# Cross-attention latent queries: from float32 matmuls to three float32r matmuls on split operands, with a new order in the loop

## The reference

```python
def _L1_xattn_ref(hidden_q, kv_c, Wq, w_kc_q, w_kc_kv, W_qr, W_kr, Wo):
    B, S, L = (2, 128, 128)
    DIM_Q, H, K, D_C, D_CQ, R = (256, 16, 128, 64, 192, 64)
    ...
    q_hk = (hidden_q @ Wq.T).reshape(Bv, Sv, H, K)
    q_big = jnp.einsum('bshk,hkq->bshq', q_hk, w_kc_q)
    ...
    q_big = _apply_rope(q_big, sin_q[None, :, None, :], cos_q[None, :, None, :])
    ...
    kv_r = _apply_rope(kv_c, sin_k[None], cos_k[None])
    q_r = jnp.einsum('bshq,hqr->bhsr', q_big, W_qr)
    k_r = jnp.einsum('bld,hdr->bhlr', kv_r, W_kr)
    scores = jnp.einsum('bhsr,bhlr->bhsl', q_r, k_r)
    attn = jax.nn.softmax(scores, axis=-1)
    ctx_c = jnp.einsum('bhsl,bld->bhsd', attn, kv_r)
    ctx_lat = jnp.einsum('bhsd,hkd->bhsk', ctx_c, w_kc_kv)
    ctx = ctx_lat.transpose(0, 2, 1, 3).reshape(Bv, Sv, H * K)
    return ctx @ Wo.T
```

## Time and profile before

| | |
|---|---|
| median of 3 runs | 1042.09 us (1037.66 to 1042.62) |
| profiled execution | 1034.71 us, its span 1032.9 us |
| PE busy in the span | 947.3 us (92%) |
| DVE, ACT, POOL busy | 633.0 us (61%), 437.7 us (42%), 113.8 us (11%) |
| mean granted clock of TensorE | 0.967 |
| latent-query matmuls | 384 records, 92.4 us |
| cross-attention set-up and loop | about 518 to 806 us of the span |

### The profile page before, as it was taken

One profiled execution on the slowest core, in us unless ns is written; L12 is line 12 of the kernel. 1 busy time (PEld: TensorE's weight loads), 2 busy tenths in 40 slices (PEclk: granted clock), 3 DMA queues, 4 the chain that ended last, 5 costly groups with the idle time before them and its releaser, 6 DMA issues.

```text
span 1032.9 us, 14127 instructions
## 1 busy us (share of the span) xinstructions
PE 947.3 (92%) x5344; PEld 735.2 (71%) x5344; DVE 633.0 (61%) x1222; ACT 437.7 (42%) x1036; POOL 113.8 (11%) x126
## 2 busy tenths in 40 slices
PE   5999779999999988888788999999998799999998
PEld 4666457888888777656476777777775578888886
DVE  4357655666566553455566867868776456666664
ACT  4722443433334313666534444434444533334432
POOL 1300000000000046000031322222221000000000
PEclk9989869999999989988999999999999899999999
DMA  5000031111110040000060000000000312111101
GB/s 215 1 2 1 1 109 46 46 51 56 46 30 1 0 163 1 2 1 2 1 275 1 2 1 1 2 1 1 2 1 1 122 33 62 47 46 46 30 1 41
DMA packets 12089, 38.37 MB, mean 37 GB/s; under 512 B 1888, under 2 KB 3968, under 8 KB 11136
## 3 DMA queue, kind: packets, MB, share of 16 engines
q1 hardware_dynamic: 12000, 37.60, 10.7%
q0 software_dynamic: 32, 0.01, 0.0%
HBM read 36.55 MB, written 1.05 MB: 36 GB/s over the span
## 4 chain that ended last, share of the span: by engine, by line
PE 73%; ACT 8%; DVE 5%; issue 1%; POOL 0%; DVEq 0%
PE ps L1005 68%; ACT Q L840 3%; PE ps L1455 2%; PE ps L1110 1%; DVE nm L482 1%; ACT probs_q L917 1%; ACT whi L855 1%; DVE stats L384 1%; DVE X L589 1%; ACT L874 0%; ACT silu_g L874 0%; ACT L917 0%; PE ps L1243 0%; PE ps L1135 0%; DVE rope_buf L649 0%
## 5 line engine op out<-in xcount | busy, mean ns | idle before, releaser
L879 ACT ACTIVATE h_hi<-weighted_h 128x512 fp32r<-128x512 f32 x100 | 63.2, 632 | 152.3 <-DVE weighted_h L575 152.3
L1005 PE MATMUL ps<-xTh,whi 128*128 128x512 f32 x400 | 125.2, 394 | 2.2 <-ACT silu_g L874 2.2
L1005 PE MATMUL ps<-xTh,wlo 128*128 128x512 f32 x400 | 123.9, 391 | 0.0
L1005 PE MATMUL ps<-xTl,whi 128*128 128x512 f32 x400 | 123.2, 389 | 0.0
L577 DVE TENSOR_TENSOR h_lo<-weighted_h,h_hi 128x512 fp32r<-128x512 f32 x100 | 69.3, 693 | 69.8 <-ACT h_hi L879 69.8
L572 DVE TENSOR_TENSOR shared_gate<-silu_g,row_shares 128x512 f32<-128x512 f32 x88 | 60.9, 692 | 64.7 <-ACT silu_g L874 64.6
L1005 PE MATMUL ps<-xT,merged_q 128*128 128x256 f32 x384 | 92.4, 384 | 1.7 <-DVE rope_buf L650 1.7
L874 ACT ACTIVATE silu_g<-ps 128x512 f32<-128x512 f32 x100 | 59.6, 596 | 79.2 <-PE ps L1005 78.9
L1005 PEld LDWEIGHTS ps<-xTh,whi 128*128 128x128 f32 x400 | 74.5, 189 | 21.5 <-issue 5.5
L997 POOL TENSOR_TENSOR latent_rot<-rope_buf 128x256 f32<-128x256 f32 x96 | 68.6, 736 | 190.7 <-DVE rope_buf L650 190.7
L1005 PEld LDWEIGHTS ps<-xTh,wlo 128*128 128x128 f32 x400 | 75.7, 189 | 15.9
(11 more groups left out here) (181 smaller groups left out, 1639.4 us busy)
## 6 DMA issues: line engine op xcount, KB each, us to landing
raw<-in_ffn SPq DMA_DIRECT2D x50, 384.0 KB, 3.1
wx<-in_wx SPq DMA_DIRECT2D x4, 2048.0 KB, 10.0
cx<-in_cx SPq DMA_DIRECT2D x1, 1536.0 KB, 9.7
wqkv<-in_wqkv SPq DMA_DIRECT2D x1, 1280.0 KB, 10.4
X<-in_x SPq DMA_DIRECT2D x4, 256.0 KB, 3.5
rope_buf<-in_kvc SPq DMA_DIRECT2D x1, 1024.0 KB, 4.7
out<-X SPq DMA_DIRECT2D x4, 256.0 KB, 2.3
cst<-in_const SPq DMA_DIRECT2D x1, 773.0 KB, 7.8
```

The costliest lines, as they stand in the source:

```text
L879: a.activation(h_hi[:, u % 2, :], weighted_h[:, u % 2, :], ACT.Copy).then_inc(act_hi[l], 1)
L1005: return pe.matmul(o, l, r, start=start, stop=stop, skip_group_check=True)
```

## The change

The latent queries' operands, merged_q and the transposed tokens, are each kept as two float32r tiles: ScalarE's copy now writes the rounded part (merged_qh, cxTh), and VectorE subtracts it from PSUM into the remainder (merged_ql, cxTl), both in the set-up; TensorE's waits for the banks go to the new semaphores merged_q_rest and cxt_rest. Each product of an LQ becomes three float32r matmuls. In the loop TensorE does LQ(w+1,1) right behind the first scores, and the output between the two transposes; VectorE takes rope(w+1,1) before its first copy; ScalarE does its first exponentials before its first copy. The tiles of both attentions are given back before cross, so that the new tiles can lie there (all ten `sb` lines of that block get `c=a_ctx`; one is shown).

```diff
--- before.py
+++ after.py
@@ -105,16 +105,16 @@
-        wqkv0 = sb("wqkv0", [P, 3, KD, D])
...
+        wqkv0 = sb("wqkv0", [P, 3, KD, D], c=a_ctx)
...
@@ -177,10 +177,14 @@
             y_sb = sb("y_sb", [P, 2, 2, HALF], c=phase)
 
 
+        a_ctx.close()
         phase = ExitStack()
         with phase:
 
-            merged_q = sb("merged_q", [P, GROUPS, KD, 2, 4 * LO], c=phase)
+            merged_qh = sb("merged_qh", [P, GROUPS, KD, 2, 4 * LO], F32R, c=phase)
+            merged_ql = sb("merged_ql", [P, GROUPS, KD, 2, 4 * LO], F32R, c=phase)
+            cxTh = sb("cxTh", [P, KD, NB, SEQ], F32R, c=phase)
+            cxTl = sb("cxTl", [P, KD, NB, SEQ], F32R, c=phase)
             merged_s = sb("merged_s", [P, GROUPS, 2, 4, 128], c=phase)
             merged_o = sb("merged_o", [P, GROUPS, 2, D], c=phase)
             cx = sb("cx", [P, CX_W], c=phase)
@@ -195,8 +199,6 @@
             sums = sb("sums", [P, 2, 2, 2], c=phase)
             rsum = sb("rsum", [P, 2, 2, 2], c=phase)
             probs_q = sb("probs_q", [P, 2, 2, 2, 2, SEQ], c=phase)
-            probs_t = sb("probs_t", [P, 2, 2, 512], c=phase)
-            contexts_sb = sb("contexts_sb", [P, 2, SEQ], c=phase)
             with ExitStack() as weights:
                 wx = sb("wx", [P, 2, XPACK], c=weights)
 
@@ -204,6 +206,8 @@
             kvh = sb("kvh", [P, NB, SEQ], F32R, c=phase)
             kvl = sb("kvl", [P, NB, SEQ], F32R, c=phase)
             tSl = sb("tSl", [P, 2, SEQ], F32R, c=phase)
+            contexts_sb = sb("contexts_sb", [P, 2, SEQ], c=phase)
+            probs_t = sb("probs_t", [P, 2, 2, 512], c=phase)
 
         def kx(name):
             a, b = CX[name]
@@ -237,6 +241,7 @@
          probs_scaled, pe_probs_t, probs_t_by_vector, probs_t_by_scalar, operand_lo, kv_hi, kv_lo, xprobs_done, pe_contexts, sums_inverted, contexts_copied, pe_xout) = map(sem, (
             "x_zeroed", "kv_products", "kv_rotated", "pe_kv_tokens", "kv_tokens_copied", "pe_merged_q", "merged_q_copied", "pe_merged_s", "merged_s_copied", "pe_merged_o", "merged_o_copied", "pe_latent", "rope_products", "latent_rotated", "pe_operand",
             "operand_hi", "pe_xscores", "xmax_done", "probs_scaled", "pe_probs_t", "probs_t_by_vector", "probs_t_by_scalar", "operand_lo", "kv_hi", "kv_lo", "xprobs_done", "pe_contexts", "sums_inverted", "contexts_copied", "pe_xout"))
+        merged_q_rest, cxt_rest = sem("merged_q_rest"), sem("cxt_rest")
         ld_loaded = sem("ld_loaded")
         pad_ready = sem("pad_ready")
         pe_ffn_xt, xt_hi, xt_lo, pe_logits, logits_copied, pe_logits_tok, logits_shifted, logits_exp, router_steps, pe_combine_t, combine_hi, combine_lo = map(
@@ -663,6 +668,13 @@
                         v.wait_ge(cx_in, 16)
                         for j in range(3):
                             rope(0, j)
+                    for jj in range(4):
+                        cols = slice(LO * jj, LO * jj + LO)
+                        v.wait_ge(merged_q_copied, 4 * hg + jj + 1)
+                        v.tensor_tensor(merged_ql[:, hg, :, :, cols], ps[:, jj, 0:2 * XQ].rearrange("p (k h f) -> p k h f", k=KD, h=2),
+                                        merged_qh[:, hg, :, :, cols].bitcast(F32), ALU.subtract).then_inc(merged_q_rest, 1)
+                    v.wait_ge(xt_ready, 8 + hg + 1)
+                    v.tensor_tensor(cxTl[:, :, hg, :], ps[:, 7, :].rearrange("p (k s) -> p k s", k=KD), cxTh[:, :, hg, :].bitcast(F32), ALU.subtract).then_inc(cxt_rest, 1)
                     v.wait_ge(x_zeroed, hg + 1)
                     for part in range(2):
                         v.wait_ge(pe_merged_s, 2 * hg + part + 1)
@@ -714,11 +726,10 @@
                     if more:
                         rope(w + 1, 0)
                     row_max(w, 0)
-                    if w >= 1:
-                        copy_transposed(w - 1, 0)
                     if more:
                         rope(w + 1, 1)
                     if w >= 1:
+                        copy_transposed(w - 1, 0)
                         copy_transposed(w - 1, 1)
                     row_max(w, 1)
                     normalise_probs(w, 0)
@@ -899,12 +910,12 @@
                 for hg in range(GROUPS):
                     for jj in range(4):
                         a.wait_ge(pe_merged_q, 4 * hg + jj + 1)
-                        a.activation(merged_q[:, hg, :, :, LO * jj:LO * jj + LO], ps[:, jj, 0:2 * XQ].rearrange("p (k h f) -> p k h f", k=KD, h=2),
+                        a.activation(merged_qh[:, hg, :, :, LO * jj:LO * jj + LO], ps[:, jj, 0:2 * XQ].rearrange("p (k h f) -> p k h f", k=KD, h=2),
                                      ACT.Copy).then_inc(merged_q_copied, 1)
                     a.wait_ge(pe_merged_o, hg + 1)
                     a.activation(merged_o[:, hg, :, :].rearrange("p e n -> p (e n)"), ps[:, 6, :], ACT.Copy).then_inc(merged_o_copied, 1)
                     a.wait_ge(pe_xt, 8 + hg + 1)
-                    a.activation(xT4[:, :, hg, :], ps[:, 7, :].rearrange("p (k s) -> p k s", k=KD), ACT.Copy).then_inc(xt_ready, 1)
+                    a.activation(cxTh[:, :, hg, :], ps[:, 7, :].rearrange("p (k s) -> p k s", k=KD), ACT.Copy).then_inc(xt_ready, 1)
                 a.wait_ge(kv_rotated, 1)
                 a.activation(kvh[:, :, :], kvT[:, :, :], ACT.Copy).then_inc(kv_hi, 1)
 
@@ -929,10 +940,9 @@
                 for w in range(UNITS):
                     a.wait_ge(pe_operand, w + 1)
                     a.activation(tSh[:, :, :].rearrange("p e s -> p (e s)"), ps[:, 2, :], ACT.Copy).then_inc(operand_hi, 1)
+                    exponentials(w, 0)
                     if w >= 1:
                         copy_transposed(w - 1, 0)
-                    exponentials(w, 0)
-                    if w >= 1:
                         copy_transposed(w - 1, 1)
                     exponentials(w, 1)
                     if w >= 1:
@@ -1348,8 +1358,9 @@
                     if n >= 2:
                         pe.wait_ge(rope_products, 2 * (n - 2) + 2)
                     for part in range(2):
-                        for kk in range(KD):
-                            last = mm(ps[:, n % 2, 256 * part:256 * part + 256], merged_q[:, hg, kk, part, 128 * tile:128 * tile + 128], xT4[:, kk, b, :], kk == 0, kk == 1)
+                        for i, (m, x) in enumerate(((merged_qh, cxTh), (merged_ql, cxTh), (merged_qh, cxTl))):
+                            for kk in range(KD):
+                                last = mm(ps[:, n % 2, 256 * part:256 * part + 256], m[:, hg, kk, part, 128 * tile:128 * tile + 128], x[:, kk, b, :], i + kk == 0, i + kk == 3)
                     last.then_inc(pe_latent, 1)
 
                 for hg in range(GROUPS):
@@ -1364,7 +1375,7 @@
 
                     for jj in range(4):
                         if hg >= 1:
-                            pe.wait_ge(merged_q_copied, 4 * (hg - 1) + jj + 1)
+                            pe.wait_ge(merged_q_rest, 4 * (hg - 1) + jj + 1)
                         if hg == 2 and jj < 2:
                             pe.wait_ge(rope_products, 6 - 2 * jj)
                         for kk in range(KD):
@@ -1385,7 +1396,7 @@
                     last.then_inc(pe_merged_o, 1)
 
                     b = hg
-                    pe.wait_ge(*((xt_ready, 8 + b) if b else (x_done, 8 * 4)))
+                    pe.wait_ge(*((cxt_rest, b) if b else (x_done, 8 * 4)))
                     pe.wait_ge(norm_done, 8 * 4 + 2 * b + 2)
                     for kk in range(KD):
                         for t in range(2):
@@ -1393,14 +1404,14 @@
                     last.then_inc(pe_xt, 1)
                     if hg == 1:
 
-                        pe.wait_ge(xt_ready, 8 + 1)
-                        pe.wait_ge(merged_q_copied, 8)
+                        pe.wait_ge(cxt_rest, 1)
+                        pe.wait_ge(merged_q_rest, 8)
                         for j in range(3):
                             latent_queries(0, j)
-                pe.wait_ge(merged_q_copied, 4 * GROUPS)
+                pe.wait_ge(merged_q_rest, 4 * GROUPS)
                 pe.wait_ge(merged_o_copied, GROUPS)
                 pe.wait_ge(merged_s_copied, 12 * GROUPS)
-                pe.wait_ge(xt_ready, 8 + NB)
+                pe.wait_ge(cxt_rest, NB)
 
                 pe.wait_ge(kv_rotated, 1)
                 for t in range(TILES):
@@ -1487,17 +1498,17 @@
                     if more:
                         latent_queries(w + 1, 0)
                     scores(w, 0)
+                    if more:
+                        latent_queries(w + 1, 1)
                     if w >= 1:
                         transposed_probabilities(w - 1, 0)
-                    if more:
-                        latent_queries(w + 1, 1)
+                    if w >= 2:
+                        output(w - 2)
                     if w >= 1:
                         transposed_probabilities(w - 1, 1)
                     scores(w, 1)
                     if more:
                         latent_queries(w + 1, 2)
```

(2 more changed lines are left out.)

## The result

The median of six runs is 1048.82 us (1043.8 to 1052.6), that of the kernel before in the same comparison 1041.36 us. The ratio is 1.008 [1.0046, 1.0115]: slower by 0.8%, more than the 0.5% that counts here as no change. The forecast, 1045 us, held the time in its range, but it gave "within 0.5%" the larger chance.

The account below looks back on a forecast made before the run. TensorE was taken to bound the loop before, with VectorE and GpSimd chains binding after. Set-up +6.9, loop ends +0.2, units -6.9, last unit -1.9 and clock +4.7 gave +3.0 us: 1045 us predicted, range 1036 to 1052.

Parts of the forecast that it names:

- Latent queries: Loop, TensorE: twelve float32r matmuls at 0.117 us, 1.42 us with border, 0.41 us less for each latent query.
- Rival 4: Latent queries: weight loads lie open under short matmuls, 2.84 us a latent query, total near 1100 us; chance 0.05.
- The two chains: Loop: two dependency chains that the longer latent queries covered now bind; waits of 0.40 and 0.14 us a unit.
- Chain (a): Loop, second scores through row maximum, scaling, rotation and GpSimd's sum to the query side's last four records: 6.34 us.
- chain (b): Loop, query side's last records through ScalarE's copy and VectorE's rest to the first scores: 2.53 us with hand-over.
- Rival 2: Loop: the chains bind less, unit 14.23 us as TensorE alone wants, total about 1036 us; chance 0.18.
- A unit: Loop: 6.34 + 2.53 + 5.85 = 14.73 us against 15.46, 0.73 us less.
- Every fourth unit: Three loop units: table load beside the scores, -0.95 us each; copy late behind the square root, +1.24 us each.
- The set-up: Before the loop: masked copies now stand behind the context-token remainder, +6.9 us, ends 4 and 8.
- The clock: Set-up and unit 0: TensorE's clock halves after idle gaps of 5.8 and 3.9 us, +4.7 us, ends 0 and 7.
- Rival 1: Set-up and unit 0: the clock holds, total 1040.3 us; chance 0.17.
- Rival 3: The low clock stays on into the loop, 3 to 6 us more, total 1048 to 1052 us; chance 0.13.

Follow-up runs that it names:

- two-term kernel: Changed kernel with the product of merged_ql and cxTh left out, 8 matmuls a latent query instead of 12: 1042.13 us in one run, unit 14.42 us.
- square: Unit times of float32 and split latent queries, each in the loop order before and the new one: 15.46, 15.50; 14.62, 14.90 us.
- early table load: Changed kernel plus a one-column exponential on ScalarE right behind the copy tSh in units 6, 10 and 14: 1045.91 us in one run.
- gaps filled: Changed kernel plus 24 and 16 useless float32r matmuls on TensorE at the set-up's two waits: 1042.16 us, ratio 1.0026 to the kernel before.
- second experiment: Changed kernel with the loop orders of all three engines put back as before, split and new set-up kept: 1040.17 us, ratio 1.002 to the kernel before.

## Why the prediction was right in most of its mechanisms and low in its sum

**Latent queries.** 0.12 us a matmul against 0.117: right, and the trace has the 576 records. Rival 4 is out. What a whole latent query saves was not right; see the unit below. The rule that was weighed, in the Trainium skill's page "TensorE: Matmul & The Clock Gate", Part 3, does not hold here: each of these matmuls has a weight load of its own over the same 128 rows, and they follow one another every 0.12 us.

**The two chains.** Shown by GpSimd's row, by the wait in front of the scores and by the two-term kernel, which saved 0.48 us of 1.44. Chain (a) was to take 6.34 us, and takes 645.37 - 639.02 = 6.35 from the second scores to the last four records of the query side; chain (b) took 2.54 instead of 2.53. So the chains' lengths were right. What they cost was not: TensorE's own way under chain (a) is 6.22 us (6.35 less the wait of 0.13) and not 5.94. Rival 2 is out, but its 14.23 was out of reach in any order: 14.62 is what the kernel with the order before takes, in which the query side does not wait. What the forecast said of the output's place is the square's content: before, the output stood inside chain (a) and covered it, and the new order took it out. With float32 queries the rest still covers the chain (0.04 us lost); with the split it doesn't (0.28 lost).

**A unit: the term that was mis-sized.** The forecast took 1.32 us for the latent query between scores and transposes, by subtraction from a float32 one. It is 1.54: twelve matmuls at 0.12, and its first pair, behind scores on half the rows, takes 0.34 us instead of 0.24. The forecast had dropped this border, which its own rows show (1.83 us for a latent query behind scores, 1.73 for one behind transposes), and then subtracted it once more: 1.32 is less than its own 12 x 0.117 = 1.40. The part in line takes 6.01 us instead of 5.85, 0.17 in the unit, 13 x 0.17 = 2.2 us.

That only 0.17 us are missing is luck. Three latent queries were to save 1.23 us and saved 15.46 - 14.62 = 0.84 with the order before, 0.28 each on average and not 0.41; the waits of the new order were to take back 0.50 and took 0.28. The two errors have one root: with latent queries longer than forecast, TensorE comes later to each wait. Of the 0.39 us that the queries did not save, 0.22 came back as shorter waits.

**Every fourth unit: the step that failed.** "With the exponentials first, the load runs beside the scores." It does not: the load waits for the row maximum and then for nothing else. The forecast had 1.24 us a unit, measured 1.87; 3 x 0.63 = 1.9 us. The early table load gave that back and left 1.21, so the other half of the step, the square root, was right. (The idle time in the row of the second transposes is 0.47; by the starts TensorE loses 0.63.) A plausible reason is that the first exponential waits for two semaphores, sums_inverted and xmax_done, and the load comes between these waits; in unit 0, where it has one wait fewer, the load starts at 575.12, right behind tSh, and the square root, which waits for norm_var alone, has its load at 659.04, ahead of that wait. This was seen in three places and not tried by itself. Of the load, the Trainium skill says, page "ScalarE: Activation LUTs", section on what ACT_TABLE_LOAD costs, that it takes about 1283 ns and that a drain of about 1380 ns is added at every switch. The 1.28 us agree; of the drain nothing is seen, neither behind the load, where the exponential starts after 0.02 us, nor ahead of it in the early load, which starts 0.02 us after tSh has ended.

**The set-up.** The order was to cost 6.9 us. Of the measured 10.6 some 3.45 are low clock: 1.2 on latent query 2, 1.85 on group 2 (7.66 instead of 5.81 us), 0.4 on the keys. So 7.1 are the order's: right, and with the gaps filled it is 7.0. The clock's share was to be 2.1: group 2 was hit harder than the 0.8 assumed. That part is chance in either direction: the same code cost group 2 nothing in the second experiment's profile and 2.0 us in that of the early table load.

**The clock.** It fell behind both stalls, as forecast, and it costs 6.2 us by the filled gaps, where the forecast had 4.7 and 7 as the upper end. The query side of unit 0 lost 5.12 - 2.66 = 2.46 us (forecast 2.6). Rival 1 is out. Rival 3 had the measured time in its range (1048 to 1052), but not for its reason: the loop's units run at full rate from unit 1 on.

**The sum.** +3.0 was forecast for cross and +9.2 measured. Of the 6.2 missed, 4.1 are in the units (2.2 + 1.9), 1.6 in the set-up, almost all of it the clock on group 2, and 0.5 in small pieces. The three errors that count had the same sign: each term was priced as if what the new operation meets (a partner on half the rows, a wait ahead of the table load, a clock that stays low for longer) did not exist. The split itself was worth its price: with the loop's order before, a better order in the set-up and the early table load it is 11.5 us of cross, some 8 of them its own. Both rearrangements that came with it were losses: 7.0 us in the set-up, without its low clock, and 6.8 in the loop.

## What to carry to other kernels

When a part of the bounding engine's work gets shorter, ask first what it had covered: here GpSimd and VectorE chains of 6.35 and 2.54 us lay under it, and the order which covers them must be chosen again after the gain, not before. In a set-up, put the copy that the bounding engine waits for ahead of one which itself waits for a third engine. And price a stall of the matmul engine with the low clock behind it: two stalls of 5.69 and 3.87 us cost another 6.2 us in work behind them, and 1.85 less in another execution of the same set-up.

## What the runs showed of the hardware that was not expected

- Forty superfluous matmuls made the kernel faster, 6.2 us of cross: TensorE kept its 2.4 GHz through two waits.
- The clock fell behind a stall of 3.95 us, and group 2 was slow (7.49 us instead of 5.81) even when the stalls were 1.05 and 1.94 us. Yet it ran at full clock (5.81 us) in one execution with stalls of 5.69 and 1.47 us, and at 0.54 of it for 4 us (7.66 us in all) in another with the same two stalls.
- A function table's load does not run ahead of every wait: at 665.83 it started with the row maximum, after 2.60 us of idle time. Another, at 659.04 in the same unit, started 3.42 us before its instruction did.
- A float32r pair behind matmuls on half the rows took 0.34 us, one behind its like 0.24.
- The same code reached the cross stage between 518.5 and 530.2 us in ten profiled executions. A difference of two spans says little about a change of 10 us; the length of the changed stage says more.
